# Edge loop of a graph network: the products by the scalar features of two tiles in one VectorE instruction, and VectorE two tiles ahead of its additions instead of three

## Chip, cores and metric

One core of one Trainium2 chip. Times are device microseconds (us) of a whole execution of the kernel; those of single instructions are in us or ns. Lower is better.

## What is computed

Four graph layers over 1250 nodes of 512 features, and 21250 edges sorted by their receiver. Only the second layer has a loop that the change touches:

```python
x0, x1 = _lin_irreps(x0, x1, W_up0, W_up1)
h = edge_feats
for W in (W_mlp1, W_mlp2, W_mlp3):
    h = SILU_2MOM * jax.nn.silu(h @ W / jnp.sqrt(jnp.float32(W.shape[0])))
tpw = h @ W_mlp4 / jnp.sqrt(jnp.float32(W_mlp4.shape[0]))
w1, w2, w3, w4 = jnp.split(tpw, 4, axis=-1)
s0 = x0[sender]
s1 = x1[sender]
p1 = w1 * s0 * y0
p2 = (w2 * s0)[:, :, None] * y1[:, None, :]
p3 = w3[:, :, None] * s1 * y0[:, None, :]
p4 = w4 * jnp.einsum('eum,em->eu', s1, y1) / SQRT3
msg0 = jax.ops.segment_sum(m0, receiver, num_segments=num_nodes)
msg1 = jax.ops.segment_sum(m1, receiver, num_segments=num_nodes)
```

Each edge takes the 512 features of its sender: 128 scalar ones (s0) and 128 vectors of three (s1). It multiplies them by weights of its own, and the messages m0 and m1 are summed at the receiver.

## The kernel before

**Tiles.** The edges lie in 208 tiles of 128, one edge to a partition, and every tile's receivers fall into one block of 32 nodes. Eight tiles are a group (TP = 8). The main loop takes two groups, that is 16 tiles, in each of 12 passes, and a 13th pass is written out behind it. Every engine runs this loop by itself, in an order written by hand, and semaphores tie them together.

**The work on one tile m**, by engine and line:

- GpSimd, L688: an indirect DMA (the gather) fetches the senders' rows into slot m % 8 of `ring`. Two gathers are issued when `s_prod_ok` says that both slots' earlier contents were used. Once in eight tiles L680 and L681 copy the group's indices and records, with `s_gidx_ok` behind them.
- TensorE, L1046 (`tpw`): the edge weights of two tiles into two of the PSUM banks 0, 1, 6, 7, with `s_tpw_ps` behind each. It waits until the tile that used the bank before has its products.
- VectorE, L1930: once in four tiles, the unscaled one-hots of four tiles (`s_eq_ok`). ScalarE, L1486: four scaled one-hots for each tile (`s_sel_ok`); it waits for `s_scat_done` of the tile four before.
- VectorE, `products`: L1938, the scalar features by two of the four weights (128 x 256), and L1939, the vector features by the other two (128 x 768), with `s_prod_ok` behind it. `prod` has four slots.
- TensorE, L1060 (`scat`): eight matmuls (16 instructions) that sum the tile's products by receiver into bank 2 + m % 4. It waits for `s_prod_ok` and `s_sel_ok`, and sets `s_scat_done`.
- VectorE, L1947 (`add_sums`): adds this PSUM result to the block's rows of `acc`. It waits for `s_scat_done` of tile m, and for the end of the addition before. The waits stand ahead of the register instructions that work out the address.

**Orders.** VectorE: products of tile m + 3 (AHEAD = 3), then the addition of tile m. TensorE: weights of pair k + 1, then `scat` of tiles 2k and 2k + 1. Nothing else than the addition's wait keeps VectorE from overwriting a slot of `prod` that TensorE still reads: the slot of tile m + 3 is the one that tile m - 1 used, and the addition of m - 1 stands right ahead.

Of the kernel before, what the change touches and what calls it, by code (L numbers as in the profile page):

```python
# [9 lines left out]
MUL, HID = 128, 64  # L10
# [22 lines left out]
TP = 2 * GT  # L33
# [10 lines left out]
NDG = G // 2  # L44
DGB = 4
NSM = 17
AHEAD = 3
assert NB % WR == 0 and G % 4 == 0
HB = NB // 2
assert E + NDB * 127 <= NT * 128 and G % 4 == 0  # L50
# [33 lines left out]
def build(nc, a, out):  # L84
# [4 lines left out]
    ALU = mybir.AluOpType  # L89
# [3 lines left out]
    with ctx:  # L93
# [6 lines left out]
        def sem(name):  # L100
            return ctx.enter_context(nc.semaphore(name))
# [39 lines left out]
        def at(off, shape, dt=f32):  # L141

            size = int(np.prod(shape[1:]))
            words = size if dt in (f32, f32r, i32, u32) else (size + 1) // 2
            assert off + words <= ARENA
            v = arena[:shape[0], off:off + words]
            if dt != f32:
                v = v.bitcast(dt)
            if len(shape) == 3:
                v = v.rearrange("p (a b) -> p a b", a=shape[1])  # L150
            if len(shape) == 4:
                v = v.rearrange("p (a b c) -> p a b c", a=shape[1], b=shape[2])
            return v

        PS = ctx.enter_context(nc.psum_tensor("PS", [128, 8, 512], f32))
# [88 lines left out]
        ring = at(10240, [128, 2 * GT, D])  # L244
        xT1 = at(14336, [128, KT, N])
        xup_st = at(19500, [NP, 2, D])
        prod = at(14336, [128, 4, 8 * MUL])
# [143 lines left out]
        s_tpw_ps = sem("s_tpw_ps")  # L391
# [43 lines left out]
        s_gath = [sem(f"s_gath{k}") for k in range(2 * GT)]  # L435
# [1128 lines left out]
        def _(dve):  # L1564
            v = nc.vector
# [47 lines left out]
            m = NDB  # L1613
# [41 lines left out]
            m = NBK  # L1655
# [263 lines left out]
            dve.sem_inc(s_sel_ok, 2 * TP)  # L1919
            dve.sem_inc(s_gsum_ok, 4)  # L1920

            def products(m, par, n, n_pair, n_gath):

                s = m % 4
                if m == 0:
                    dve.wait_ge(s_gidx_ok, n_pair)
                if m % 4 == 0:
                    dve.wait_ge(s_sel_ok, n + (2 * TP - 4))
                    dl = gslot[:, par, :].rearrange("p (t k) -> p t k", k=RW)[:, m:m + 4, R_DL:R_DL + 1]
                    v.tensor_tensor(eq4[:, m // 4, :].rearrange("p (t n) -> p t n", t=4),  # L1930
                                    iota_dst[:, 0:DB].unsqueeze(1).to_broadcast([128, 4, DB]),
                                    dl.to_broadcast([128, 4, DB]), ALU.is_equal).then_inc(s_eq_ok, 1)
                xg = ring[:, m, :].rearrange("p (q n) -> p q n", q=4)
                w = PS[:, (0, 1, 6, 7)[s], :].rearrange("p (q n) -> p q n", q=4)
                pr = prod[:, s, :].rearrange("p (h q n) -> p h q n", h=2, q=4)
                dve.wait_ge(s_gath[m], n_gath)
                dve.wait_ge(s_tpw_ps, n + (2 - m % 2))
                v.tensor_tensor(pr[:, :, 0, :], w[:, 0:3:2, :], xg[:, 0:1, :].to_broadcast([128, 2, MUL]), ALU.mult)  # L1938
                v.tensor_tensor(pr[:, :, 1:4, :], w[:, 1:4:2, :].unsqueeze(2).to_broadcast([128, 2, 3, MUL]),  # L1939
                                xg[:, 1:4, :].unsqueeze(1).to_broadcast([128, 2, 3, MUL]), ALU.mult).then_inc(s_prod_ok, 1)  # L1940

            def add_sums(m, n, word):
                b = ((word >> (6 * (m % 4))) & 63).with_bounds(min_val=0, max_val=NDB - 1)
                dve.wait_ge(s_scat_done, n + 5)
                dve.wait_ge(s_gsum_ok, n + 4)
                d = acc[:, bass.ds(b * 256, 256)]
                v.tensor_tensor(d, PS[:, 2 + m % 4, 0:256], d, ALU.add).then_inc(s_gsum_ok, 1)  # L1947

            def two_groups(i, par, last=False):
                for m in range(TP):  # L1950
                    if m + AHEAD < TP:
                        products(m + AHEAD, par, i * (2 * TP) + (TP * par + m + AHEAD), None, i * 32 + 16 * (par + 1))
                    elif not last:
                        products(m + AHEAD - TP, 1 - par, i * (2 * TP) + (TP * par + m + AHEAD), i * 2 + (par + 2),
                                 i * 32 + 16 * (par + 2))
                    if m % 4 == 0:
                        word = dve.value_load(gpk[0:1, m // 4, bass.ds(i * 2 + par, 1)], min_val=0, max_val=64 ** 4 - 1)
                    add_sums(m, i * (2 * TP) + (TP * par + m), word)
            products(0, 0, 0, 1, 16)
            products(1, 0, 1, None, 16)  # L1960
            products(2, 0, 2, None, 16)
            with dve.Fori(0, G // 4 - 1) as i:
                two_groups(i, 0)
                two_groups(i, 1)
            two_groups(G // 4 - 1, 0)
            two_groups(G // 4 - 1, 1, last=True)
            dve.wait_ge(s_gsum_ok, NT + 4)
# [134 lines left out]
```

## Time and profile before

| | us |
|---|---|
| median of 3 runs | 1746.64 (1743.93 to 1747.52) |
| the profiled execution, whole | 1744.53 |
| its span, first to last instruction | 1742.6 |
| edge loop, first gather to last addition | 725.2 to 1086.8 |
| VectorE busy in the span | 1321.9 (76%) |
| TensorE matmuls busy in the span | 1470.6 (84%) |

The profile is of one execution. A row of the timeline gives the start, the duration, the engine and line, and in square brackets how long the engine had been idle before it and what ended that. "PE" is TensorE's matmuls, "PEld" its weight loads, "DVE" VectorE, "ACT" ScalarE, "POOL" GpSimd. The ends of matmuls are modelled, so that only their starts, and what other engines wait for, tell when they were done. VectorE's instructions overlap by some 0.08 us: the next one starts before the former one's end.

### The profile page before, as it was taken

Reading aid. Unit: us, or ns where it says so; the run is one execution under the profiler, and the core shown is the slowest. Engines: PE = TensorE matmul, PEld = TensorE weight load, DVE = VectorE, ACT = ScalarE, POOL = GpSimd, SP = SyncE. Lnnn points to the kernel's source line nnn. Section 1 sums busy time; section 2 is a strip of 40 time slices with the busy share of each in tenths; the row PEclk is TensorE's granted clock in tenths of the full one; section 3 lists DMA queues with packets and bytes.
Section 4 is the critical chain, followed back from the end, with each engine's and each line's share of the span. In section 5 each row is a group of like instructions: output and inputs, shape, how many; then the busy total and the mean of one; then the engine's idle time right before and its main releaser. Section 6 shows DMA issues by size and latency. Waiting matters only on the chain.

```text
span 1742.6 us, 24098 instructions
## 1 busy us (share of the span) xinstructions
PE 1470.6 (84%) x7759; PEld 794.3 (46%) x7759; DVE 1321.9 (76%) x2036; ACT 727.0 (42%) x1595; POOL 499.8 (29%) x490
## 2 busy tenths in 40 slices
PE   2888998174878783799999999869899989999997
PEld 1465545022433332655655555745444434444443
DVE  8796999968999998499998999788377357724232
ACT  1285664075555553455554555431244134312000
POOL 1788888700010001255665664000000000002000
PEclk9889998587999996899999999979999999999999
DMA  4101000143120201455665666001011121210000
GB/s 150 31 6 9 6 6 6 35 144 87 55 73 30 72 15 39 136 169 172 189 182 166 180 190 123 1 0 49 0 58 62 48 73 48 72 72 0 12 18 29
DMA packets 67195, 122.74 MB, mean 70 GB/s; under 512 B 12613, under 2 KB 31159, under 8 KB 67010
## 3 DMA queue, kind: packets, MB, share of 16 engines
q0 software_dynamic: 22944, 58.12, 13.3%
q1 hardware_dynamic: 42748, 59.87, 10.6%
q10 hardware_dynamic: 1446, 4.03, 0.7%
q8 instruction: 30, 0.49, 0.1%
q14 instruction: 27, 0.22, 0.0%
HBM read 106.57 MB, written 15.22 MB: 70 GB/s over the span
## 4 chain that ended last, share of the span: by engine, by line
PE 48%; DVE 19%; POOL 14%; issue 11%; ACT 4%; DMA 3%; DVEq 1%; SPq 0%; ACTq 0%; another core or an unknown queue 0%; POOLq 0%
PE PS L1175 18%; POOL recs L641 14%; PE PS L1060 7%; DVE arena L1811 6%; PE PS L1223 5%; PE PS L1143 5%; PE PS L1046 4%; DVE arena L1807 3%; ACT arena L1486 2%; PE PS L1219 2%; PE PS L1211 2%; DVE arena L1775 2%; DVE arena L1947 1%; PE PS L1111 1%; DVE cnt_d L1581 1%
## 5 line engine op out<-in xcount | busy, mean ns | idle before, releaser
L1175 PE MATMUL PS<-arena 128*125 128x512 f32 x720 | 314.4, 600 | 12.1 <-ACT arena L1545 6.6
L641 POOL DMA_INDIRECT recs<-arena x170 | 249.0, 1464 | 90.6 <-issue 90.0
L1486 ACT ACTIVATE arena<-arena,gslot 128x32 f32<-128x32 f32 x832 | 185.3, 308 | 170.9 <-DVE arena L1930 81.6
L1060 PE MATMUL PS<-arena 128*32 128x128 f32 (+1 forms) x3328 | 231.3, 308 | 18.4 <-issue 7.9
L688 POOL DMA_INDIRECT arena<-xup,gidx x208 | 197.6, 950 | 141.8 <-DVE arena L1939 62.0
L1060 PEld LDWEIGHTS PS<-arena 128*32 128x32 f32 x3328 | 174.5, 110 | 127.5 <-issue 73.3
L977 PE MATMUL PS<-arena 125*128 125x512 f32 (+1 forms) x480 | 190.6, 535 | 44.0 <-DVE arena L1811 44.0
L1175 PEld LDWEIGHTS PS<-arena 128*125 128x125 f32 x720 | 136.8, 190 | 189.2 <-issue 189.2
L1939 DVE TENSOR_TENSOR arena<-PS,arena 128x768 f32<-128x768 f32 x208 | 196.7, 946 | 0.0
L695 POOL CAST arena<-cnt_s 125x1250 f32<-125x1250 uint16 x10 | 12.6, 1303 | 495.3 <-PE PS L1175 495.3
L977 PEld LDWEIGHTS PS<-arena 125*128 125x128 f32 x480 | 86.1, 192 | 148.5 <-issue 78.2
L1438 ACT ACTIVATE arena<-arena,c 125x1250 f32<-125x1250 f32 x80 | 106.8, 1337 | 101.3 <-DVE arena L1807 101.2
L1807 DVE SCALAR_TENSOR_TENSOR arena<-arena,c 125x1250 f32<-125x1250 f32 x90 | 135.8, 1512 | 8.7 <-ACT arena L1401 7.5
L1046 PE MATMUL PS<-arena 64*128 64x512 f32 x416 | 122.1, 658 | 2.3 <-issue 2.1
L1811 DVE SCALAR_TENSOR_TENSOR arena<-arena,cnt_s 125x1250 f32<-125x1250 f32 x80 | 116.1, 1453 | 0.0
L1938 DVE TENSOR_TENSOR arena<-PS,arena 128x256 f32<-128x256 f32 x208 | 86.5, 416 | 21.4 <-remote 10.9
L1324 ACT ACTIVATE arena<-PS 125x626 uint16<-125x626 f32 x104 | 70.0, 692 | 54.2 <-PE PS L849 38.3
L1947 DVE TENSOR_TENSOR arena<-PS,arena 128x256 f32 x208 | 85.8, 412 | 7.8 <-remote 6.7
L1143 PE MATMUL PS<-arena,x_sb 125*128 125x512 f32 (+1 forms) x240 | 86.0, 520 | 5.0 <-DVE arena L1811 5.0
L1223 PE MATMUL PS<-arena 125*125 125x512 f32 x200 | 87.5, 592 | 0.0
L849 PE MATMUL PS<-arena 128*125 128x512 bf16 (+1 forms) x416 | 73.9, 311 | 9.9 <-DVE arena L1720 7.5
L1550 ACT ACTIVATE arena<-arena,cslot 128x2500 f32<-128x2500 f32 x16 | 38.1, 2382 | 103.0 <-DVE cslot L2032 103.0
(311 smaller groups left out, 2008.2 us busy)
## 6 DMA issues: line engine op xcount, KB each, us to landing
arena<-in_spline_wT SPq DMA_DIRECT2D x16, 1024.0 KB, 5.3
arena<-uv_rows SPq DMA_DIRECT2D x14, 610.4 KB
arena<-h_rows SPq DMA_DIRECT2D x26, 256.0 KB
h_rows<-arena SPq DMA_DIRECT2D x24, 256.0 KB, 2.8
arena<-xup,gidx POOLq DMA_INDIRECT x208
recs<-arena POOLq DMA_INDIRECT x170
xup<-arena SPq DMA_DIRECT2D x10, 250.0 KB
out<-x_sb SPq DMA_DIRECT2D x10, 250.0 KB
```

The source lines that it names most:

```text
L641: pool.indirect_dma_start(out=recs, out_offset=bass.IndirectOffsetOnAxis(pos[:, c:c + 1], 0), in_=rec[:, c, :], in_offset=None).then_inc(s ...
L688: pool.indirect_dma_start(out=ring[:, m, :], out_offset=None, in_=xup, in_offset=bass.IndirectOffsetOnAxis(gidx[:, par, m:m + 1], 0))\
L977: ins = t.matmul(PS[:, 3 * par + q, 0:n1 - n0], hs[:, sblk, par * C:par * C + 2 * C], wt[:, sblk % WR, n0:n1], start=(sblk == 0), stop=(sb ...
L1046: t.matmul(PS[:, tpw_bank[(2 * k + q) % 4], :], h3[r, buf, k * 128:(k + 1) * 128], w_m4[r, :], start=True, stop=True, tile_position=(q * H ...
L1060: ins = t.matmul(PS[quad * DB:(quad + 1) * DB, bank, o0 * MUL:o0 * MUL + w], sel4[:, s, v * DB:(v + 1) * DB], prod[:, s, c0 * MUL:c1 * MUL ...
L1143: ins = t.matmul(PS[:, b0 + q, 0:n1 - n0], w, P50[:, k, n0:n1], start=(k == 0), stop=(k == NB - 1))
L1175: ins = t.matmul(PS[:NP, b, :], basis[:, slot, (k * HB + b) * NP:(k * HB + b + 1) * NP], w_sp[:, slot, k * D:(k + 1) * D], start=(first an ...
L1223: ins = t.matmul(PS[:NP, b % 2, :], cnt50[:, k, b * NP:(b + 1) * NP], z_sb[:, k, :], start=(k == 0), stop=(k == NB - 1))
L1486: ins = A(sel4[:, s, y * DB:(y + 1) * DB], eq4[:, m // 4, s * DB:(s + 1) * DB], ACT.Copy, scale=gslot[:, par, c + R_Y + y:c + R_Y + y + 1])
L1807: v.scalar_tensor_tensor(dst, U, cc, V, ALU.add, ALU.max).then_inc(ok, 1)
L1811: v.scalar_tensor_tensor(dst, e, 1.0, cm, ALU.min, ALU.mult).then_inc(ok, 1)
L1939: v.tensor_tensor(pr[:, :, 1:4, :], w[:, 1:4:2, :].unsqueeze(2).to_broadcast([128, 2, 3, MUL]), xg[:, 1:4, :].unsqueeze(1).to_broadcast([1 ...
```

## The change

`products` is cut in two. `scalar_products(m)` is called for even m and does tiles m and m + 1 in one instruction of 128 x 512 over the two neighbouring banks; it first waits for both gathers and for the weights of both tiles. `vector_products(m)` is what L1939 was. VectorE goes two tiles ahead of the additions instead of three. The additions, and the loops of the other engines, are left as they are.

```diff
-AHEAD = 3
-            def products(m, par, n, n_pair, n_gath):
+            def scalar_products(m, par, n, n_pair, n_gath):
...
+                bank = (0, 1, 6, 7)[s]
+                w2 = PS[:, bank:bank + 2, :].rearrange("p t (h q n) -> p t h q n", h=2, q=2)
+                pr2 = prod[:, s:s + 2, :].rearrange("p t (h q n) -> p t h q n", h=2, q=4)
+                dve.wait_ge(s_gath[m], n_gath)
+                dve.wait_ge(s_gath[m + 1], n_gath)
+                dve.wait_ge(s_tpw_ps, n + 2)
+                v.tensor_tensor(pr2[:, :, :, 0, :], w2[:, :, :, 0, :],
+                                ring[:, m:m + 2, 0:MUL].unsqueeze(2).to_broadcast([128, 2, 2, MUL]), ALU.mult)
+
+            def vector_products(m):
+                s = m % 4
...
-                dve.wait_ge(s_gath[m], n_gath)
-                dve.wait_ge(s_tpw_ps, n + (2 - m % 2))
-                v.tensor_tensor(pr[:, :, 0, :], w[:, 0:3:2, :], xg[:, 0:1, :].to_broadcast([128, 2, MUL]), ALU.mult)
...
                 for m in range(TP):
-                    if m + AHEAD < TP:
-                        products(m + AHEAD, par, i * (2 * TP) + (TP * par + m + AHEAD), None, i * 32 + 16 * (par + 1))
+                    if m + 2 < TP:
+                        if m % 2 == 0:
+                            scalar_products(m + 2, par, i * (2 * TP) + (TP * par + m + 2), None, i * 32 + 16 * (par + 1))
+                        vector_products(m + 2)
...
-            products(0, 0, 0, 1, 16)
-            products(1, 0, 1, None, 16)
-            products(2, 0, 2, None, 16)
+            scalar_products(0, 0, 0, 1, 16)
+            vector_products(0)
+            vector_products(1)
```

In the changed kernel L1938 is the double scalar product, L1946 the vector product, L1929 the one-hots and L1954 the addition.

The head of the loop on VectorE, before: the one-hots of tiles 0 to 3, the products of tiles 0, 1 and 2, then those of tile 3 as the first of the loop.

```order
L1930 TENSOR_TENSOR arena<-iota_dst,gslot 128x128 [waits s_xup_cp,s_x_ok,s_acc_zero,s_sel_ok,s_gidx_ok]
L1938 TENSOR_TENSOR arena<-PS,arena 128x2x128 [waits s_tpw_ps,s_gath0]
L1939 TENSOR_TENSOR arena<-PS,arena 128x2x384
L1938 TENSOR_TENSOR arena<-PS,arena 128x2x128 [waits s_tpw_ps,s_gath1]
L1939 TENSOR_TENSOR arena<-PS,arena 128x2x384
L1938 TENSOR_TENSOR arena<-PS,arena 128x2x128 [waits s_tpw_ps,s_gath2]
L1939 TENSOR_TENSOR arena<-PS,arena 128x2x384
...
L1938 TENSOR_TENSOR arena<-PS,arena 128x2x128 [waits s_tpw_ps]
L1939 TENSOR_TENSOR arena<-PS,arena 128x2x384
```

And now: the double scalar product of tiles 0 and 1, their two vector products, then the double scalar product of tiles 2 and 3, and the vector product of tile 2.

```order
L1929 TENSOR_TENSOR arena<-iota_dst,gslot 128x128 [waits s_xup_cp,s_x_ok,s_acc_zero,s_sel_ok,s_gidx_ok]
L1938 TENSOR_TENSOR arena<-PS,arena 128x4x128 [waits s_tpw_ps,s_gath1,s_gath0]
L1946 TENSOR_TENSOR arena<-PS,arena 128x2x384 x2
...
L1938 TENSOR_TENSOR arena<-PS,arena 128x4x128 [waits s_tpw_ps]
L1946 TENSOR_TENSOR arena<-PS,arena 128x2x384
```

The first instruction now waits for two gathers, and one tile less has its products when the first addition comes.

A stretch within a group on VectorE, before: products of tile 5, addition of tile 2 (its waits stand in the register row with `s_scat_done`), products of tile 6, addition of tile 3.

```order
L1938 TENSOR_TENSOR arena<-PS,arena 128x2x128 [waits s_tpw_ps,s_gath5]
L1939 TENSOR_TENSOR arena<-PS,arena 128x2x384
L1944 REGISTER_ALU
L1947 REGISTER_ALU [waits s_gsum_ok,s_scat_done]
...
L1947 TENSOR_TENSOR arena<-PS,arena 128x256
L1937 REGISTER_ALU [waits s_gath6]
L1938 TENSOR_TENSOR arena<-PS,arena 128x2x128 [waits s_tpw_ps]
L1939 TENSOR_TENSOR arena<-PS,arena 128x2x384
L1947 REGISTER_ALU [waits s_gsum_ok,s_scat_done]
...
L1947 TENSOR_TENSOR arena<-PS,arena 128x256
```

The same place now: addition of tile 2, vector product of tile 5, addition of tile 3, then the double scalar product of tiles 6 and 7 and the vector product of tile 6.

```order
L1954 TENSOR_TENSOR arena<-PS,arena 128x256
L1946 TENSOR_TENSOR arena<-PS,arena 128x2x384
L1951 REGISTER_ALU
L1954 REGISTER_ALU [waits s_gsum_ok,s_scat_done]
...
L1954 TENSOR_TENSOR arena<-PS,arena 128x256
L1938 TENSOR_TENSOR arena<-PS,arena 128x4x128 [waits s_tpw_ps,s_gath7,s_gath6]
L1946 TENSOR_TENSOR arena<-PS,arena 128x2x384
```

The addition of tile 3 came behind the products of tile 6; now it comes right behind the vector product of tile 5, and the scalar products of tiles 6 and 7 come behind it. The same holds for every odd tile and the pair three above it.

## Rows read from the trace of the kernel before

**Rows 1.** The page: span, and the costliest VectorE groups of the loop.

```profile
span 1742.6 us, 24098 instructions
L1939 DVE TENSOR_TENSOR arena<-PS,arena 128x768 f32<-128x768 f32 x208 | 196.7, 946 | 0.0
L1938 DVE TENSOR_TENSOR arena<-PS,arena 128x256 f32<-128x256 f32 x208 | 86.5, 416 | 21.4 <-remote 10.9
L1947 DVE TENSOR_TENSOR arena<-PS,arena 128x256 f32 x208 | 85.8, 412 | 7.8 <-remote 6.7
```

**Rows 2.** Stretches: length, busy PE, PEld, DVE, ACT, POOL; clock, DMA share, GB/s.

```profile
941.00:1073.00 132.00, 127.68 (x1457) 78.44 (x1451) 129.05 (x263) 72.16 (x324) 80.94 (x101) 1.00 0.68 181
806.00:833.00 27.00, 24.94 (x266) 14.77 (x264) 23.17 (x49) 12.66 (x57) 14.94 (x18) 0.94 0.58 167
914.00:941.00 27.00, 24.15 (x245) 14.81 (x243) 21.32 (x46) 10.68 (x48) 13.07 (x16) 0.87 0.50 150
```

**Rows 3.** Timeline of one group of four tiles in the steady part.

```profile
959.22 0.94 DVE L1939 TENSOR_TENSOR arena<-PS,arena 128x768 f32<-128x768 f32 x1
960.29 0.82 PEld L1060 LDWEIGHTS PS<-arena 128*32 128x32 f32 x16 [0.39 <-issue]
960.42 0.28 DVE L1930 TENSOR_TENSOR arena<-iota_dst,gslot 128x128 f32<-128x128 f32 x1
...
960.62 0.41 DVE L1938 TENSOR_TENSOR arena<-PS,arena 128x256 f32<-128x256 f32 x1
960.92 0.94 POOL L688 DMA_INDIRECT arena<-xup,gidx  x1 [0.81 <-DVE arena L1939]
960.95 0.94 DVE L1939 TENSOR_TENSOR arena<-PS,arena 128x768 f32<-128x768 f32 x1
961.31 1.13 PE L1046 MATMUL PS<-arena 64*128 64x512 f32 x4
...
962.17 0.95 POOL L688 DMA_INDIRECT arena<-xup,gidx  x1 [0.30 <-issue]
962.48 0.94 DVE L1939 TENSOR_TENSOR arena<-PS,arena 128x768 f32<-128x768 f32 x1
963.34 0.41 DVE L1947 TENSOR_TENSOR arena<-PS,arena 128x256 f32 x1
...
963.81 0.96 ACT L1486 ACTIVATE arena<-arena,gslot 128x32 f32<-128x32 f32 x4 [0.35 <-PE PS L1060]
963.90 0.42 DVE L1938 TENSOR_TENSOR arena<-PS,arena 128x256 f32<-128x256 f32 x1
...
966.96 0.28 DVE L1930 TENSOR_TENSOR arena<-iota_dst,gslot 128x128 f32<-128x128 f32 x1
```

**Rows 4.** Timeline of ScalarE alone, 941 to 1075 us.

```profile
944.20 0.96 ACT L1486 ACTIVATE arena<-arena,gslot 128x32 f32<-128x32 f32 x4 [0.38 <-PE PS L1060]
...
954.28 3.50 ACT L1486 ACTIVATE arena<-arena,gslot 128x32 f32<-128x32 f32 x16 [3.04 <-DVE arena L1930]
...
1068.54 0.96 ACT L1486 ACTIVATE arena<-arena,gslot 128x32 f32<-128x32 f32 x4 [0.35 <-PE PS L1060]
```

**Rows 5.** Timeline of the loop's end, behind the last gather.

```profile
1073.51 0.95 POOL L688 DMA_INDIRECT arena<-xup,gidx  x1 [0.31 <-issue]
...
1076.54 0.41 DVE L1938 TENSOR_TENSOR arena<-PS,arena 128x256 f32<-128x256 f32 x1
...
1082.85 0.41 DVE L1938 TENSOR_TENSOR arena<-PS,arena 128x256 f32<-128x256 f32 x1
...
1084.05 0.41 DVE L1947 TENSOR_TENSOR arena<-PS,arena 128x256 f32 x1
...
1084.82 0.42 DVE L1947 TENSOR_TENSOR arena<-PS,arena 128x256 f32 x1 [0.36 <-DVE arena L1947]
```

**Rows 6.** TensorE alone, where it runs without a pause.

```profile
936.82 1.95 PE L1060 MATMUL PS<-arena 128*32 128x256 f32 x32
```

**Rows 7.** Timeline of the loop's head.

```profile
735.30 0.42 DVE L1947 TENSOR_TENSOR arena<-PS,arena 128x256 f32 x1 [1.23 <-remote]
```

More of the change, by code:

```diff
@@ L1950, in two_groups @@
                 for m in range(TP):
-                    if m + AHEAD < TP:
-                        products(m + AHEAD, par, i * (2 * TP) + (TP * par + m + AHEAD), None, i * 32 + 16 * (par + 1))
+                    if m + 2 < TP:
+                        if m % 2 == 0:
+                            scalar_products(m + 2, par, i * (2 * TP) + (TP * par + m + 2), None, i * 32 + 16 * (par + 1))
+                        vector_products(m + 2)
                     elif not last:
-                        products(m + AHEAD - TP, 1 - par, i * (2 * TP) + (TP * par + m + AHEAD), i * 2 + (par + 2),
-                                 i * 32 + 16 * (par + 2))
+                        if m % 2 == 0:
+                            scalar_products(m + 2 - TP, 1 - par, i * (2 * TP) + (TP * par + m + 2), i * 2 + (par + 2),
+                                            i * 32 + 16 * (par + 2))
+                        vector_products(m + 2 - TP)
                     if m % 4 == 0:
```

## The prediction

> **What bounds the kernel now.** I read the page first, then the busy time by stretches, then the timeline of one group of four tiles, line by line, and at last ScalarE's timeline alone, since it waits for the same signals as VectorE's additions.
>
> The page gives VectorE 208 scalar products of 416 ns, 208 vector products of 946 ns and 208 additions of 412 ns [rows 1]. In the steady part of the edge loop VectorE is busy 129.05 of 132 us and TensorE 127.68 [rows 2]. The ends of TensorE's rows are modelled, so I look for its floor where it runs without a pause: two tiles' matmuls take 1.95 us [rows 6], and their weights' matmuls 1.13 [rows 3], together 3.08 us for a pair of tiles at most. A group of four tiles takes 966.96 - 960.42 = 6.54 us [rows 3], 3.27 for a pair. TensorE has 0.19 to spare.
>
> VectorE's own work: behind the last gather, where it waits for nothing, the same point of the order comes again after 1082.85 - 1076.54 = 6.31 us [rows 5]. So 0.23 us of the 6.54 is waiting. It is seen at 963.90: the addition of 963.34 needs 0.33, yet the next scalar product starts 0.56 behind it [rows 3], for the weights of its pair.
>
> What a slot costs, start to next start, from the same rows [rows 3]: scalar product 0.33 (960.62 to 960.95), vector product 0.86 (962.48 to 963.34), one-hots 0.20 (960.42 to 960.62), addition 0.41 less the overlap of 0.08, which is 0.33.
>
> **When TensorE's signals arrive.** Call q the tile of the group's one-hots. The vector product of tile q-1 ends at 959.22 + 0.94 = 960.16; TensorE starts on it at 960.29 and has loaded its sixteen weights by 961.11. The scaled one-hots of tile q+3 wait for this tile's `s_scat_done`. They start at 963.81, after 0.35 of idle time put down to TensorE: the signal came 3.65 us behind the end of the product, though the matmuls were issued 2.7 us before [rows 3]. The weights issued at 961.31 show the same: they are used at 963.90. Both come some 0.7 behind the end of the second gather (962.17 + 0.95 = 963.12), which that same product let go. Behind the last gather, VectorE's wait is gone [rows 5]. I take it that signals are held while GpSimd gathers; for the sum only the 3.65 counts.
>
> How often? In ScalarE's timeline from 941 to 1069 us, 12 of 20 groups show this break, twelve activations and then four behind an idle time near 0.35; in the other 8 all sixteen run through [rows 4].
>
> The Trainium skill says otherwise (TensorE: Matmul & The Clock Gate, "The cost: per-tile semaphore tail"): a semaphore increment on the last matmul comes some 56 ns behind it. That does not agree with the 963.81 of this trace. By the page the addition would never wait; this is rival C below.
>
> **What the change does, part by part.**
>
> *One instruction for two.* From 256 to 768 columns the duration grows by 946 - 416 = 530 ns, 1.035 ns a column, so 512 columns take 681 ns, a slot of 0.60 against two of 0.33: 0.07 less for a pair, 0.14 for four tiles, 7.3 us over 52 groups. Bounds: 0.53 (two widths of 0.265, no start-up at all) and 0.66 (no gain). I take 0.60, the line between two measured widths. The multiplications and their operands stay, and the waits it adds (the second gather, the second tile's weights) are for things that came together before, since the gathers are issued eight tiles ahead.
>
> *Two tiles ahead.* The addition of an odd tile now stands right behind the vector product of two tiles later. I set the end of the product of q-1 to 0 and lay out the new order with the slots: addition q-3 at -0.08, one-hots 0.25, double scalar product 0.45, vector product q 1.05, addition q-2 1.91, vector product q+1 2.24. The addition of q-1 could start at 3.10. Its signal comes at 3.65. Its wait stands ahead of the register instructions; their time no row shows alone. It lies between 0 and the 0.36 that lies between two chained additions [rows 5]; I take 0.20, near the middle. So it starts at 3.85: a wait of 0.75. Behind it are queued the double scalar product (4.18), vector product q+2 (4.78), addition q (5.64) and vector product q+3 (5.97, ends 6.91). With that product the next gathers and TensorE's next tile are let go, so the cycle is 6.91 us for four tiles. The odd tile between, q+1, ends at 3.18 and would be signalled for 7.03 against its slot of 6.83: this 0.20 lies under the next wait.
>
> Before, the same addition stood behind the product of tile q+2, at 963.90 + 0.33 + 0.86 = 965.09, 1.28 behind the signal [rows 3]. That was the cover, and it is gone.
>
> *Sum.* A held group goes from 6.54 to 6.91, +0.37. One with no signal held is VectorE's own work, 6.31 - 0.14 = 6.17, -0.37. Each cycle has two odd tiles; if each is held 12 times in 20, both are free 0.4 x 0.4 = 0.16 of the time. 52 x 0.37 x (0.84 - 0.16) = +13.1 us.
>
> *Head and tail.* The first double product waits for one gather more, but the first addition stands until 735.30 for a signal that comes with the gathers' end [rows 7]; nothing is added. At the end three chained additions follow the last product instead of four: 0.77 (1084.05 to 1084.82) [rows 5] less the 0.33 of a slot is 0.4 us less. ScalarE, SyncE and GpSimd keep their orders; GpSimd's gathers follow the products as before.
>
> The profiled execution took 1744.53 us, 1.9 outside its span. 1744.5 + 13.1 - 0.4 = 1757.2, and the median of the runs is 2.1 above that execution: **1759 us**.
>
> **Rivals.**
>
> *A, the forecast: the odd additions wait.* Bounds: no register time gives a cycle of 6.71, 52 x (0.84 x 0.17 - 0.16 x 0.37) = +4.3, or 1751; every group held with 0.36 of register time gives 7.07, +27.6, or 1774. Two stretches of the loop are disturbed now: VectorE is busy 23.17 and 21.32 in 27 us against 26.4 in steady ones [rows 2], 8.3 us lost together. They may go, or come twice: 8 us either way. For it: ScalarE's rows. Chance 0.62.
>
> *B, the addition finds its signal there, and only the merge counts.* This ends on the other side. It needs the signal before 2.9 instead of at 3.65 (the slot at 3.10 less the 0.20), as in the 8 groups that run through, for instance if the gathers shift with the new order. The wait of 0.23 for weights stays: -7.3 - 0.4, so 1739 us. Chance 0.17.
>
> *C, signals come at once everywhere.* All waits go: 52 x 0.37 = 19.2 and 0.4 less, 1727 us. Against it are the waits of rows 3. Chance 0.05. It is the skill's rule, as above.
>
> *D, the two balance.* If half of the groups are held, 52 x 0.37 x (0.5 - 0.5) = 0: between 1743 and 1750. Chance 0.11.
>
> *E, TensorE is disturbed more often.* Longer pauses bring the granted clock down, as in the disturbed stretches (0.94 and 0.87 against 1.00) [rows 2]. One such stretch of 4.2 us in each of 13 passes instead of two in all: 46 us on top, 1805. It decides once a pause of VectorE outlasts TensorE's 0.19 to spare by several us; 0.75 does not. Chance 0.05.
>
> **Numbers.** A measurement here can tell about 0.2%, 3.5 us. Faster: B and C, 0.22. The same: D, 0.11. Slower: A and E, 0.67. The range goes from B's 1739, with a us below it, to A's upper bound and a little of the disturbed stretches, 1776; it leaves out C, E and the ends of A, about 0.15. A alone would have 1751 to 1776.
>
> **What the profile after would show.** The double scalar product at 681 ns, 104 times, and VectorE idle ahead of L1954, put down to L1060, 0.5 to 1 us at odd tiles, some 30 to 50 times: A. Hardly any idle time there, and still 0.2 ahead of L1938: B. No idle time in VectorE at all: C. The period from one set of one-hots to the next: 6.9 (A), 6.4 (B), 6.17 (C). I am wrong if the signals of odd tiles follow their own matmuls instead of coming 3.65 behind the product, since then the time given up by the shorter lead costs nothing.

## The result, and the profile after

The changed kernel takes **1770.74 us** (median of 4 runs, 1759.92 to 1773.72) against 1747.08 for the kernel before (4 runs beside them, 1743.93 to 1748.0). The ratio is 1.0137, 95% interval 1.011 to 1.0164. The forecast had the direction (slower) and the engine that waits; its loss, 12 us on the median, is about half of the 24 measured. The profiled execution took 1769.92 us.

The page of the changed kernel, which answers to [rows 1]: busy us and mean ns of one, then the idle time ahead of the group.

```profile
span 1768.0 us, 23974 instructions
L687 POOL DMA_INDIRECT arena<-xup,gidx x208 | 197.5, 950 | 171.2 <-DVE arena L1946 101.7
L1946 DVE TENSOR_TENSOR arena<-PS,arena 128x768 f32<-128x768 f32 x208 | 196.8, 946 | 0.0
L1954 DVE TENSOR_TENSOR arena<-PS,arena 128x256 f32 x208 | 86.5, 416 | 52.1 <-remote 26.5
```

The groups of the stretch from 700 to 1110 us have the double scalar product, too:

```profile
L1938 DVE TENSOR_TENSOR arena<-PS,arena 128x512 f32<-128x512 f32 x104 | 71.1, 683 | 10.8 <-DMA arena<-xup,gidx 5.9 <-remote 4.1 <-PE PS L1045 0.2
```

The double product lasts 683 ns (681 were forecast). Idle time ahead of the additions grew from 7.8 to 52.1 us: +44.3. Ahead of the scalar products it fell from 21.4 to 10.8: -10.6. The merge takes 0.14 for each group of four tiles: -7.3. Together +26.4, and the span grew by 1768.0 - 1742.6 = 25.4. So the loss is idle time ahead of the additions.

The head of the loop is in these sums and is no part of the loss. In the changed kernel the first two additions wait 2.99 and 2.38 us there; in the kernel before the first addition waits 1.23 and the fifth scalar product, at 742.33, waits 6.41. From the first one-hots to the third it is 23.4 us now and was 24.2.

The waits of VectorE from 735 to 1100 us: us in total, times, longest.

```profile
DVE arena L1954 <- PE PS L1059: 23.9, 19, 2.4
DVE arena L1954 <- remote: 23.5, 19, 3.4
DVE arena L1938 <- remote: 4.1, 8, 0.9
```

And the stretch in which the kernel before had its two disturbances: the granted clock is 1.00 over all of it, so that nothing of the loss in it is TensorE's clock.

```profile
741.00:1090.00 349.00, 318.40 (x3438) 188.42 (x3435) 300.46 (x526) 169.21 (x762) 191.56 (x240) 1.00 0.57 164
```

**Which additions wait.** VectorE's timeline shows by the next row which tile an addition belongs to. 22 waiting additions stand ahead of a double scalar product: tile q-1, the forecast's, 27.9 us in all. 20 stand ahead of a vector product: the even tiles, 20.7 us (q 13 times with 14.8, q-2 7 times with 5.9). 4 stand ahead of the one-hots: tile q+1, 2.8 us, of which 2.38 is the wait in the head. Two more, 0.36 each, stand between and behind the chained additions of the loop's end. One group of the changed kernel with both kinds of odd tile:

```profile
958.04 0.95 DVE L1946 TENSOR_TENSOR arena<-PS,arena 128x768 f32<-128x768 f32 x1
...
959.23 0.28 DVE L1929 TENSOR_TENSOR arena<-iota_dst,gslot 128x128 f32<-128x128 f32 x1
959.74 0.95 POOL L687 DMA_INDIRECT arena<-xup,gidx  x1 [0.74 <-DVE arena L1946]
960.99 0.95 POOL L687 DMA_INDIRECT arena<-xup,gidx  x1 [0.30 <-issue]
961.23 0.94 DVE L1946 TENSOR_TENSOR arena<-PS,arena 128x768 f32<-128x768 f32 x1
962.88 0.42 DVE L1954 TENSOR_TENSOR arena<-PS,arena 128x256 f32 x1 [0.70 <-PE PS L1059]
...
965.01 0.95 DVE L1946 TENSOR_TENSOR arena<-PS,arena 128x768 f32<-128x768 f32 x1
966.09 0.42 DVE L1954 TENSOR_TENSOR arena<-PS,arena 128x256 f32 x1
966.43 0.28 DVE L1929 TENSOR_TENSOR arena<-iota_dst,gslot 128x128 f32<-128x128 f32 x1
```

The product of q-1 ends at 958.99, and its addition starts at 962.88, after 0.70 of waiting: 3.89 behind (3.85 and 0.75 were forecast). The addition of q+1 at 966.09 should have started at 965.01 + 0.86 = 965.87; it has 0.22 of delay, too little for the profile to name it. The forecast had seen this 0.20 and let it lie "under the next wait". But the next group waits nowhere. The group took 966.43 - 959.23 = 7.20 us where 6.91 was forecast.

The other kinds are not in the forecast at all. First a late signal of an even tile, in VectorE's timeline:

```profile
931.77 0.94 DVE L1946 TENSOR_TENSOR arena<-PS,arena 128x768 f32<-128x768 f32 x1
936.12 0.42 DVE L1954 TENSOR_TENSOR arena<-PS,arena 128x256 f32 x1 [3.40 <-remote]
936.46 0.95 DVE L1946 TENSOR_TENSOR arena<-PS,arena 128x768 f32<-128x768 f32 x1
```

In GpSimd's timeline five gathers stand in this wait, one behind another, and the last of them ends at 934.79, 1.33 us ahead of the addition; the first and the last:

```profile
928.83 0.94 POOL L687 DMA_INDIRECT arena<-xup,gidx  x1 [2.07 <-issue]
...
933.84 0.95 POOL L687 DMA_INDIRECT arena<-xup,gidx  x1 [0.30 <-issue]
```

Then two of tile q-1, later than the 3.85 of the forecast:

```profile
897.53 0.95 DVE L1946 TENSOR_TENSOR arena<-PS,arena 128x768 f32<-128x768 f32 x1
897.68 1.73 PEld L1059 LDWEIGHTS PS<-arena 128*32 128x32 f32 x32 [0.76 <-issue]
...
903.32 0.42 DVE L1954 TENSOR_TENSOR arena<-PS,arena 128x256 f32 x1 [1.65 <-PE PS L1059]
```

```profile
852.42 0.95 DVE L1946 TENSOR_TENSOR arena<-PS,arena 128x768 f32<-128x768 f32 x1
...
858.98 0.42 DVE L1954 TENSOR_TENSOR arena<-PS,arena 128x256 f32 x1 [2.42 <-PE PS L1059]
```

They start 4.84 and 5.61 us behind their product's end. So the lateness is no constant. Of the 50 groups behind the first one, 15 take less than 6.3 us, and 20 take 7.6 or more, up to 9.7, mostly in turn.

**The signal is late, not the matmuls.** The trace also records each time that a semaphore was counted up; here the counts of `s_scat_done` are matched to the tiles in order (one of 208 is missing in the changed kernel's trace, two in that of the kernel before). For the addition at 903.32, TensorE has loaded the last weights of the tile by 899.41 (row of 897.68), 0.94 us behind the product. The count is recorded at 903.03, and the addition starts 0.29 behind it. How many of the 52 tiles of each kind have their count more than 2.9 us behind the end of their own product:

| | q-1 | q | q+1 | q-2 |
|---|---|---|---|---|
| kernel before | 29 | 5 | 21 | 7 |
| changed kernel | 26 | 20 | 21 | 9 |

The odd tiles are late about as often as before; what changed for them is the cover. Tile q, which was late 5 times, is late 20 times in the changed kernel, nearly always in the same groups in which the odd tiles are late, and 19 times by more than 4.5 us. At some of these the last matmul starts 1.7 us behind the product, where 1.0 is usual for q; the rest is the signal. The shorter lead as a loss of cover does not explain that: the change also moved the signals themselves, and why is not shown.

### The profile page after: what moved, and what is told of

Its sections match the earlier page's. It is cut to its first block, busy times and chain, and to the rows that moved or that the text cites. A ratio compares the mean times of both kernels' runs of the same rounds, so it can differ in the third digit from the quotient of the medians.

```text
span 1768.0 us, 23974 instructions
## 1 busy us (share of the span) xinstructions
PE 1484.8 (84%) x7759; PEld 792.8 (45%) x7759; DVE 1317.0 (74%) x1932; ACT 725.9 (41%) x1595; POOL 495.9 (28%) x490
## 4 chain that ended last, share of the span: by engine, by line
PE 52%; DVE 24%; issue 9%; ACT 6%; DMA 3%; DVEq 2%; another core or an unknown queue 2%; SPq 0%; POOL 0%; ACTq 0%; POOLq 0%
PE PS L1174 18%; DVE arena L1810 6%; PE PS L1059 6%; PE PS L1142 5%; PE PS L1222 5%; DVE arena L1774 4%; DVE arena L1806 3%; PE PS L1045 3%; PE PS L848 2%; ACT arena L1267 2%; PE PS L762 2%; PE PS L1210 2%; DMA x_sb<-in_x 2%; PE PS L1218 2%
## 5 line engine op out<-in xcount | busy, mean ns | idle before, releaser
L640 POOL DMA_INDIRECT recs<-arena x170 | 245.1, 1442 | 90.4 <-issue 90.1
L1059 PE MATMUL PS<-arena 128*32 128x128 f32 (+1 forms) x3328 | 240.6, 306 | 35.5 <-DVE arena L1946 16.9
L1946 DVE TENSOR_TENSOR arena<-PS,arena 128x768 f32<-128x768 f32 x208 | 196.8, 946 | 0.0
L1954 DVE TENSOR_TENSOR arena<-PS,arena 128x256 f32 x208 | 86.5, 416 | 52.1 <-remote 26.5
L848 PE MATMUL PS<-arena 128*125 128x512 bf16 (+1 forms) x416 | 74.9, 313 | 10.6 <-DVE arena L1719 8.5
L2074 DVE TENSOR_SCALAR arena<-PS,deg 125x512 f32<-125x512 f32 x10 | 7.5, 752 | 97.0 <-PE PS L1222 97.0
```

The costliest lines, as they stand in the source:

```text
L640: pool.indirect_dma_start(out=recs, out_offset=bass.IndirectOffsetOnAxis(pos[:, c:c + 1], 0), in_=rec[:, c, :], in_offset=None).then_inc(s ...
L1059: ins = t.matmul(PS[quad * DB:(quad + 1) * DB, bank, o0 * MUL:o0 * MUL + w], sel4[:, s, v * DB:(v + 1) * DB], prod[:, s, c0 * MUL:c1 * MUL ...
```

## The experiments

They ran on four chips. The chip of the pair above, from here on the first pair, is not on record, so that they differ from it in the chip or only in the time. Beside them the kernel before took 1714 to 1722 us, some 30 less than in the first pair; runs 5 and 6 are on this.

**1. The shorter lead alone.**

```diff
-AHEAD = 3
+AHEAD = 2
...
-            products(2, 0, 2, None, 16)
```

> The shorter lead alone: VectorE two tiles ahead of the additions, the scalar products one by one as before. Theory H (TensorE's signals are held while GpSimd issues gathers, and the shorter lead puts the odd additions ahead of the held signal): the loss of the change is all the lead's, and the merge gave a few us back: 24 to 32 us over the kernel before (1771 to 1779), with VectorE idle ahead of the additions 45 to 60 us in all. Theory M (the double instruction delays things by waiting for two gathers and two tiles' weights at once, and the lead costs little): within 8 us of the kernel before.

Measured: 1716.05 us, the kernel before 1716.04 (ratio 0.9996, 0.998 to 1.0013). No loss. VectorE's idle time ahead of the additions is 0.7 us in all. Theory H fell here as I had put it.

**2. The merge alone, lead of three, `prod` with eight slots.**

```diff
-        prod = at(14336, [128, 4, 8 * MUL])
+        prod = at(14336, [128, 8, 8 * MUL])
...
-                    if m + 2 < TP:
-                        if m % 2 == 0:
-                            scalar_products(m + 2, ...)
-                        vector_products(m + 2)
+                    if m + 3 < TP:
+                        if m % 2 == 1:
+                            scalar_products(m + 3, ...)
+                        vector_products(m + 3)
```

> The merged scalar product alone, with the lead of three tiles kept (the product tile has eight slots instead of four, so that two products can be written ahead). Theory H: the additions keep their cover, idle time ahead of them stays near 8 us, and the merge brings what VectorE's widths give: 3 to 8 us under the kernel before (1739 to 1744). Theory M: the double instruction's waits cost 15 us or more even so, 1760 or above.

Measured: 1712.84 us, ratio 0.9976 (0.996 to 0.9992), 3.2 us less. The merge is worth a little.

**3 and 4. Both kernels without the gathers of the loop** (`ring` is set to ones ahead of it).

```diff
-                        pool.indirect_dma_start(out=ring[:, m, :], ...).then_inc(s_gath[m], 16)
+                        pool.sem_inc(s_gath[m], 16)
```

> The kernel before without the indirect gathers of the edge loop: GpSimd waits for the products as before and then only counts the gather's semaphore up; the ring of gathered rows holds ones throughout, so the output is not the reference's. Theory H: no gather, no held signal: the additions and the scaled one-hots find their signals, the group of four tiles falls from 6.54 to about 6.3 us, 12 to 20 us under the kernel before (1727 to 1735). Theory T (the late signals are TensorE's own: they come late for what stands in its queue): the group keeps 6.54, within 5 us of the kernel before.

> The changed kernel without the indirect gathers of the edge loop, done in the same way (the output is not the reference's). Theory H: the waits ahead of the additions are gone (under 10 us in all instead of 52) and the merge is a gain: 20 to 26 us under the kernel before (1721 to 1727), 4 to 8 us under the kernel before without its gathers. Theory T: the waits stay, and the time is still some 20 us above the kernel before without its gathers.

Measured: before 1713.79 (ratio 0.9983, 0.9968 to 0.9999), after 1706.55 (0.994, 0.9918 to 0.9961). The 12 to 20 us of theory H did not show, but not because of theory T: at this place there was no late signal to take away. The merged kernel without gathers is 7.2 us faster than the one before without gathers: the merge's full price of 7.3.

**5 and 6. Both kernels again, unaltered.**

> The changed kernel once more, unaltered, beside the kernel before on one chip. In the experiments so far the kernel before took 1716 us instead of 1747, and the shorter lead alone cost nothing. Theory P (the held signals belong to the place where a program runs: a chip or a core of it, not to the kernel): where the kernel before takes about 1716, the changed one has no waits ahead of its additions, its group of four tiles takes 6.15 to 6.2 us instead of 6.3, and it takes 4 to 10 us less than the kernel before (1706 to 1712); where the kernel before takes about 1747, it takes 20 to 27 more. Theory C (the combination of merge and shorter lead costs, though neither alone does): 15 us or more above the kernel before wherever it runs, VectorE idle ahead of its additions some 50 us.

> The kernel before once more, unaltered, for its profile. Theory P: at a time near 1716 the additions and the scalar products wait for nothing and a group of four tiles takes 6.3 us instead of 6.54; at a time near 1747 the breaks of the rows ahead of the prediction are there again. Theory C makes no statement on it.

Measured: after 1710.93, before 1714.41, ratio 0.9984 (0.9969 to 1.0); the single execution of before 1715.83. The same changed kernel that lost 24 us is 3.5 faster here. The profiled executions, 741 to 1040 us, the one before first, then the changed one:

```profile
741.00:1040.00 299.00, 293.35 (x3421) 183.39 (x3420) 299.00 (x618) 166.97 (x765) 191.29 (x239) 1.00 0.68 192
```

```profile
741.00:1040.00 299.00, 296.72 (x3494) 187.77 (x3492) 299.00 (x533) 169.52 (x776) 193.50 (x242) 1.00 0.70 194
```

VectorE is busy for the whole 299 us in both. The waits of [rows 3] are gone from the kernel before: its group in the same part of the loop, of which the one-hots are shown, takes 966.98 - 960.67 = 6.31 us.

```profile
960.67 0.27 DVE L1930 TENSOR_TENSOR arena<-iota_dst,gslot 128x128 f32<-128x128 f32 x1
...
966.98 0.27 DVE L1930 TENSOR_TENSOR arena<-iota_dst,gslot 128x128 f32<-128x128 f32 x1
```

From the first one-hots to the last, before and after:

```profile
L1930 DVE TENSOR_TENSOR arena<-iota_dst,gslot x52: 268/270/294, 722.5 to 1049.0; 128x128 f32<-128x128 f32 x52
```

```profile
L1929 DVE TENSOR_TENSOR arena<-iota_dst,gslot x52: 268/270/292, 720.5 to 1041.5; 128x128 f32<-128x128 f32 x52
```

That is 326.5 and 321.0 us. In the first pair the same rows gave 353.8 (724.3 to 1078.1) and 382.9 (719.4 to 1102.3). So practically the whole difference between the places is in this loop, 27 us for the kernel before and 62 for the changed one. And it is late signals: in runs 5 and 6 the count of `s_scat_done` is recorded 0.29 us behind the start of the tile's last matmul in 199 of 207 and in 201 of 208 tiles; in the first pair this holds for 28 of 206 (before) and 52 of 207 (changed), and the others come up to 8.5 us behind it. Theory P stands in that lateness belongs to the place or the time and not to the kernel (which of the two is not shown), theory C is out. The gathers are the same in all (0.95 us each, 208 of them): that GpSimd gathers is not enough to make a signal late.

**7, 8 and 9. A late signal made by hand**, since no place with late ones was to be had. An odd tile's addition also waits for `s_gate`, which GpSimd counts up behind the second gather after this tile's product.

```diff
                             .then_inc(s_gath[m], 16)
+                        if m % 2 == 1:
+                            pool.wait_ge(s_gate, i * TP + (TP // 2 * par + m // 2 + 1))
+                            pool.nop(nofuse=True)
+                            pool.memset(gsc[:, 0:256], 0.0).then_inc(s_gate, 1)
...
                 dve.wait_ge(s_scat_done, n + 5)
+                if m % 2 == 1:
+                    dve.wait_ge(s_gate, n_gate)
```

(The early gate has `pool.sem_inc(s_gate, 1)` in place of the memset.)

> A held signal made by hand in the changed kernel: VectorE's addition of an odd tile also waits for a semaphore that GpSimd counts up behind the second of the two gathers that follow this tile's product, and behind a memset of 256 columns after them. The gathers start about 0.75 us behind the product's end and the second ends 2.95 behind it [rows 3]; with about 0.32 for the memset and a little for the signal the addition is let go about 3.35 us behind the product. Theory S (my sum: the addition's own place is 3.10, the registers behind the wait take 0.20, all later work shifts by the wait, once in four tiles): a group of four tiles takes 3.35 + 0.20 - 3.10 = 0.45 us more than the free 6.17, the time is 23 us above the changed kernel's 1711 (1734, with 0 to 0.36 for the registers 1724 to 1742). Theory D (both odd tiles of a group wait in full, since the gate of each lies the same way behind its own product): twice that, 1750 to 1765.

> The same without the memset: the addition of an odd tile is let go when the second gather has been issued, about 3.05 us behind its product. Theory S: 3.05 + 0.20 - 3.10 = 0.15 us for four tiles, 8 us above the changed kernel's 1711 (1719; with 0 to 0.36 for the registers 1711 to 1727). Theory D: twice that, 1727 and more.

> The late gate with its memset in the kernel before. Its odd additions stand about 4.6 us behind their product (the addition of 965.09 against the product's end at 960.16 is 4.93 in a held group), 1.2 behind the gate. Both theories: no wait, within 4 us of the kernel before (1711 to 1719). If GpSimd with its memset were the new bound, this run would be slower too, by what GpSimd takes for a pair of tiles over 3.15 us.

Measured: after with the late gate 1752.21 (ratio to the kernel before 1.0196, 1.017 to 1.0222), with the early gate 1711.12 (0.9967), before with the late gate 1721.95 (1.0032, 1.0011 to 1.0054), the kernel before 1717.49. A signal 3.3 us behind the product costs the lead of two 41 us (1752.21 - 1711.12), and the lead of three 4.5. The changed kernel's timeline under the late gate:

```profile
908.42 0.95 DVE L1956 TENSOR_TENSOR arena<-PS,arena 128x768 f32<-128x768 f32 x1
...
910.12 0.96 POOL L690 DMA_INDIRECT arena<-xup,gidx  x1 [1.23 <-DVE arena L1956]
...
911.40 0.95 DVE L1956 TENSOR_TENSOR arena<-PS,arena 128x768 f32<-128x768 f32 x1
...
912.33 0.33 POOL L696 MEMSET gsc<- 128x256 f32 x1
...
912.94 0.42 DVE L1966 TENSOR_TENSOR arena<-PS,arena 128x256 f32 x1 [0.59 <-POOL gsc L696]
...
913.28 0.28 DVE L1939 TENSOR_TENSOR arena<-iota_dst,gslot 128x128 f32<-128x128 f32 x1
```

The product ends at 909.37, the memset at 912.66, the addition starts at 912.94: 3.57 behind the product, 0.28 behind the memset. It stands ahead of the one-hots, so it is the addition of q+1, the *nearer* of the two odd ones: its own place is 911.40 + 0.86 = 912.26, 2.89 behind the product. The one of q-1 has its place at 3.10 and, pushed back by this wait, finds its gate open. The waits, us, times, longest:

```profile
DVE arena L1966 <- POOL gsc L696: 34.1, 50, 4.0
```

Once in a group, and always at q+1. A group takes 913.28 - 906.42 = 6.86 us. Theory S gave 6.62 because it counted from 3.10; from 2.89 its own sum is 6.18 + 3.57 - 2.89 = 6.86. Theory D has the time (1752) but not the mechanism: one of two waits, not both. With the early gate there is hardly a wait (2.6 us in two of them); the addition of q+1 starts 2.90 behind its product, at its own place. But the gate did not open at 3.05, as expected: its count is recorded 1.09 us behind the product. So run 8 says nothing on signals near 2.9 us; it shows that the edit costs nothing when the count comes early.

**10, 11 and 12. Lead and merge apart, under the late gate, and the better version again.** The edit is that of 7, on the kernels of 1 and 2.

> The late gate in the kernel with the shorter lead and no merged products. The changed kernel under this gate took 6.86 to 6.9 us for four tiles, with its odd addition 3.6 us behind its product, where its own place is 2.90. Theory L (it is the lead alone): here the nearer odd addition has its place at 2.96 (an addition 0.33, a scalar product 0.33, a vector product 0.86, the same three again less the last, and the overlap of 0.08) and must wait to 3.6 as well: 6.31 + 0.64 = 6.95 us for four tiles, 33 us above the 1716 of the ungated one, 1745 to 1755. Theory M (the double instruction is what makes the gate bite): under 1730.

> The late gate in the kernel with merged products and the lead of three tiles. Theory L: an odd addition stands 4.9 us behind its product, 1.3 behind the gate, no wait; 6.18 us for four tiles as without the gate, with the few us that gate and memset cost the kernel before (4.5): 1712 to 1720. Theory M: 20 us or more above the ungated one, 1735 and more.

> Merged products with the lead of three tiles once more, since it is the version that keeps both: the gain of the merge and the cover of the additions. 6.18 us for four tiles against 6.31: 52 x 0.13 = 6.6 us less in the loop, of which 3.2 were seen in the first comparison; 1708 to 1714 where the kernel before takes about 1716, some 4 to 10 us under the kernel before where it takes about 1747.

Measured: the lead of two without the merge 1754.41 (1.0209, 1.0183 to 1.0234), the merge with a lead of three 1712.17 (0.9964, 0.995 to 0.9978), the kernel before 1717.0. The waits of the first, then of the second:

```profile
DVE arena L1959 <- POOL gsc L697: 29.4, 43, 5.6
```

```profile
DVE arena L1966 <- POOL gsc L696: 3.3, 2, 2.4
```

Theory L stands, theory M is out: it is the lead, and the merge neither makes it worse nor cures it. Without the gate the merge with a lead of three takes 1709.08, ratio 0.9952 (0.9934 to 0.9971), 8 us less than the kernel before.

**13, 14 and 15. The gate at an even addition instead**, that of q-2, since 20 of the waits in the result are at even tiles.

```diff
-                if m % 2 == 1:
+                if m % 4 == 2:
                     dve.wait_ge(s_gate, n_gate)
```

> The late gate and its memset in the changed kernel, but at the even addition q-2 (the second of its group of four) in place of the odd ones: it waits for the gathers and the memset behind the product of tile q-1. In the prediction's layout this addition has its place 1.91 us behind the end of the product of q-1; the gate lets it go at 3.6. Theory L (the shorter lead took the cover of even additions too): it waits 1.7 us once in a group, 7.85 us for four tiles, 52 x 1.67 = 87 us above the ungated 1711 (1798). Theory O (only odd additions are exposed, as the forecast had it): within 10 us of 1711.

> The same in the kernel before. There the addition q-2 stands 3.18 us behind the end of the product of q-1 (963.34 against 960.16 [rows 3]), so that it waits 0.4 us: 6.7 us for four tiles, 52 x 0.4 = 21 us above the ungated 1716 (1737). Theory O: within 10 us of 1716.

> The same in the kernel with merged products and the lead of three. The place of the addition q-2 is 3.10 (the slots between are the same, with the double scalar product of 0.60 for two of 0.33), so that it waits 0.5: 6.18 + 0.48 = 6.66 us for four tiles, 25 us above the ungated 1709 to 1713 (1736). Theory O: within 10 us.

Measured: after 1797.63 (ratio 1.0444, 1.0413 to 1.0474), before 1744.47 (1.0135), merge with a lead of three 1740.69 (1.0113), the kernel before 1721.93 beside them. For the last two 1737 and 1736 were expected, from a kernel before of 1716. The changed kernel:

```profile
900.48 0.28 DVE L1939 TENSOR_TENSOR arena<-iota_dst,gslot 128x128 f32<-128x128 f32 x1
...
903.81 0.42 DVE L1966 TENSOR_TENSOR arena<-PS,arena 128x256 f32 x1 [1.58 <-POOL gsc L696]
...
908.34 0.28 DVE L1939 TENSOR_TENSOR arena<-iota_dst,gslot 128x128 f32<-128x128 f32 x1
```

The group takes 7.86 us, 7.85 were expected. Theory L stands here too: the shorter lead took 1.27 us of cover from the even addition q-2 (3.18 to 1.91), and a late signal costs the changed kernel 80 to 87 us (against its 1711 in the other runs, or 5 more, as the kernel before has them here) where it costs the kernel before 22.5. The merge with a lead of three pays 27 to 32 us for it: its place for q-2 is 3.10, also short of the gate.

## Why the direction was right and the size was not

**VectorE's widths.** 681 ns were forecast, 683 measured; a free group of 6.17, and 6.18 measured where nothing is held, against 6.31 before. Right. 7.3 us for the merge: the runs without gathers give 7.2, the one-hots' rows of the unaltered kernels 5.5, the times 3 to 8.

**The wait that goes.** 52 x 0.84 x 0.23 = 10 us were to go ahead of the scalar products. From 738 us on, the timeline of the kernel before has 43 gaps of this kind, 9.7 us: the forecast's count and size. The changed kernel has 19, of up to 1 us each, 6.6 us. So only 3 us went. What went as well are the long waits of the two disturbed stretches, 9.1 us, which the sum had left as they were and the range had put at 8.

**The addition of an odd tile waits for a late signal.** Right in place for the odd tiles, and the runs under the gate show that with a signal 3.3 us late it is the lead alone. The failing step is the size of this term, "So it starts at 3.85: a wait of 0.75", and with it the cycle of 6.91. By it 52 x 0.84 x 0.75 = 33 us were to be spent ahead of the additions; 52.1 were. Three things are in the difference:

- *The lateness was taken as one number, 3.65, from one row* [rows 3]. The additions of q-1 in the result start 3.9, 4.8 and 5.6 us behind their product in the rows above. There were fewer waits than forecast at this tile (22, not 44) and longer ones (1.27 us in the mean, not 0.75): 27.9 us of the 33. The share of 0.84 took the two odd tiles of a group to be late independently of each other. By the counts they are late together 17 times in the kernel before and 19 times in the changed one, so that 33 and 28 of 52 groups have a late odd tile, not 44.
- *Even additions were laid out as free*, at 1.91 (q-2) and 4.89 (q), with no wait. The first lies 1.27 nearer to the gathers' product than before, the second 2.90 behind its own. They waited 20 times, 20.7 us, of which 2.99 in the head. This is the bulk of what was missing: without it 52.1 would be 31.4. For q-2 runs 13 and 14 show what the shorter lead costs under a late signal; it has the smaller part, 5.9 us. For q, with 14.8, no run tried it, and there the step that failed lies deeper: the forecast took the signals of the changed kernel to be as late as those before, but the count of q is over 2.9 us behind its product 20 times instead of 5. With the lateness of before, most of these additions would have found their signal.
- *The nearer odd addition sets the cycle, not the farther.* The forecast counted from the place of q-1, 3.10, and let 0.20 at q+1 lie under the next wait. If every signal came 3.65 late, the loop through q+1 (its place 2.90) would be 6.17 + 3.85 - 2.90 = 7.12, not 6.91. Run 7 shows it: 6.86 where the forecast's rule gives 6.62. In the result itself it counts for little: outside the head 0.4 us in three waits, and parts too small to be named.

**Rivals.** B and C (faster) are what happened in the runs outside the first pair: the sum "only the merge counts" gave -7.7, and the changed kernel there took 3.5 us less than the one before. C was the rule of the Trainium skill (TensorE: Matmul & The Clock Gate, "The cost: per-tile semaphore tail"). The 56 ns of the prediction are an estimate from that section's formula with one tile and one increment. In runs 5 and 6, where VectorE has no wait for TensorE in the steady part and the count comes 0.29 us behind the start of the last matmul (whose own time is in this), nothing speaks against a short tail. In the first pair the counts do that come up to 5.8 us behind it in the changed kernel. E is out, the clock was 1.00 from 741 to 1090; the two disturbed stretches, 8.3 us, are gone from that stretch in the changed kernel's profiled execution, which is one execution each and no more.

**What stays open.** Signals were late only in the first pair. The forecast's guess, that they are held while GpSimd gathers, was never tested where they are late. For it: behind the last gather the counts come 0.29 us behind the start of their last matmul again, in both kernels, but for one. Against it: the same gathers hold nothing in the other runs, and the count for the addition at 903.32 is recorded while a gather is under way (902.41 to 903.35). This is no exception: of the counts that come more than 0.4 us behind the start of their last matmul, 40 of 173 (before) and 58 of 144 (changed) come during a gather, and gathers fill 57% and 52% of the time. So they come during a gather less often than chance would have it, but a running gather does not stop them. What is different at that place was not found, nor why the counts of tile q came later there in the changed kernel, nor whether the lead alone does that or the merge, nor whether the merged kernel with a lead of three gains there.

## What to carry to other kernels

An instruction that waits for another engine's signal has a place behind the work that the signal depends on. Write this distance down for every tile of the pattern, before and after, the even ones too: the smallest of them decides, and a shorter lead takes from all. Do not carry the lateness of each signal over from the old trace: in the first pair it changed with the order. Then change the cover and the work apart: the merge with the lead of three (`prod` with eight slots) is 8 us faster than the kernel before in run 12, and under the gate at odd tiles, which costs the lead of two 41 us, it loses 3 (at the even addition q-2 it loses 27 to 32). And measure at more than one place before believing either sign: the same two kernels stood at +24 us and at -3.5.

## What was unexpected of the hardware

- The same kernel takes 1747 us in one place and 1714 to 1722 in others, at the same granted clock (0.932 and 0.936 over the span). The difference lies in late signals: in runs 5 and 6 `s_scat_done` is counted 0.29 us behind the start of the last matmul in all but 8 and 7 tiles, and VectorE is busy for 299 of 299 us; in the first pair 2.7 to 4.4 us lie between them at the tiles q-1 whose additions wait, though their matmuls were issued as early as elsewhere.
- The recorded length of VectorE's instructions is not their pace. In the kernel before the 128 x 768 product is recorded with 946 ns in the first pair, 938 in run 6, and 987 under the late gate of run 9, where the group still takes 6.31 us.
- A count that GpSimd makes behind an indirect DMA can come before the record of this DMA begins: in run 8 the gated addition starts at 902.41 without a wait, its count is recorded at 900.60, and the gather that stands ahead of this count in the program is recorded from 901.51 to 902.46. With a memset between them (run 7) the count comes behind both.

```profile
901.51 0.95 POOL L689 DMA_INDIRECT arena<-xup,gidx  x1 [0.30 <-issue]
...
902.41 0.42 DVE L1965 TENSOR_TENSOR arena<-PS,arena 128x256 f32 x1
```
